# Another order of the jobs, and of the vector and pool work beside them, in a chain of routed feed-forward layers on one core

## The chip, the core and the metric

The kernel runs on one core of a Trainium2 chip. The metric is the device time of one execution in microseconds. Before the change it is 2493.7 us, the median of three executions (2493.61 to 2494.36).

The engines are named as the profile names them: PE (TensorE, matrix products; PEld is its weight load), DVE (VectorE), ACT (ScalarE), POOL (GpSimd) and SP (SyncE, which here only issues DMAs). Each engine works through its own list of instructions in order, and they meet by semaphores.

## The reference

64 sequences of 64 tokens with 512 features go through four layers. Layers 0, 2 and 3 have one form, with weights picked per sequence from three roles:

```python
h = gelu(x @ W_down[role] + b_down[role])       # 512 -> 256
y = x + h @ W_up[role] + b_up[role]             # 256 -> 512, residual
y = (y - mean(y)) * rsqrt(var(y) + 1e-5)
x = y * gamma[role] + beta[role]
```

Layer 1 is attention inside each sequence (512 features, one head) followed by two gelu blocks with 2048 hidden features, and a clip to [0, 1]:

```python
o = softmax(q @ k.T * scale) @ v @ Wp + bp
c = gelu(o @ cW1 + cb1) @ cW2 + cb2 + onehot(codes)
m = gelu(concat(o, c) @ mW1 + mb1) @ mW2 + mb2
x = clip(x + c + m, 0, 1)
```

All is float32. A product is computed as three products of a high and a low part (hi*hi, hi*lo, lo*hi), so each operand has to be split first: ACT copies it rounded (`_hi`), DVE subtracts (`_lo`).

## The kernel before

**Three blocks.** `first` is layer 0, then comes the core (layer 1, four passes of 1024 tokens), then `last`, layers 2 and 3 in one run of 18 jobs. `first` has 9 jobs.

**Jobs.** Sequences are sorted by role on the chip. A full job ("O") is 4 tiles of 128 tokens that all have one role, so its down weights are one matrix. A mixed job ("M") has 3 tiles, each with a role of its own; its down product (`pe_mix`) is made per tile with weights out of a table of all three roles (`wm`, split by `act_split_mixed` and `dve_split_mixed`), copied out by ACT (`act_mixed`) and turned back by PE (`pe_back`). The string `KINDS` gives the order of the kinds, here `OOOMOMOOM`, and with it job numbers, tiles in SBUF, the order of loads and the rows of each job. Jobs are numbered from 0 here; those of `last` run from 0 to 17, two rounds of the string.

**One job j, engine by engine.** The order is written out by hand in loops.
- PE: down product of j; up product of tile 0 of j-1; transposes of the inputs of j+1; up products of the other tiles of j-1. Two PSUM banks take turns for the up tiles, so the product of tile t waits until DVE has added tile t-2 to the residual (`y_done`).
- ACT: `act_moments` of j-2 (two small copies), gelu of both halves of the hidden layer, `act_norm` of the first two tiles of j-2, the hi part of the transposed inputs of j+1, the other tiles of `act_norm`, then the hi part of the down weights of j+2.
- DVE: lo part of the down weights of j+1, of the hidden halves of j, residual of tile 0 of j-1, lo part of the first half of the transposed inputs of j+1, residual of tile 1, second half, then statistics and residuals of the rest, and the aggregate.
- POOL: gathers the rows of job j+2 by indirect DMA, `pool_rstd_shift` of j-2, `pool_gain_shift` of j-3 (gamma and beta), and scatters j-3. ACT's `act_norm` waits for `pool_rstd_shift`.
- SP: down weights, the table `wm`, gains, and the inputs of the core.

**Round the edges.** At the end of `first`, PE transposes the core's inputs (`x_first`) between its last up products; ACT copies them (`xr`, `xc_hi`) once the rows of jobs 2, 3 and 4, which lie in the same SBUF, are stored. The value product of the core is copied by ACT to `x_tok`, where jobs 5 and 6 lie, so ACT first waits until their rows are stored (`for i in (4, 5)` in the scalar block, ahead of the loop over the passes). PE's second query product waits for the first two of these copies (`query`, `v_done`). In `last` the up weights of layer 3 take the place of layer 2's table `wm`, and layer 3's table is loaded after the ninth job's up products.

## Time and profile before

| what | value |
|---|---|
| median of three executions | 2493.7 us |
| profiled execution, device time | 2495.45 us |
| its span, first to last instruction | 2493.7 us |
| PE busy | 2405.3 us, 96% |
| DVE, ACT, POOL busy | 987.4, 874.2, 380.1 us |
| mean granted clock of TensorE | 0.99 |

The span is the stretch that the rows below count from; the execution's own time is 1.75 us more. In a row of the timeline the first number is the start, the second the busy time, and the bracket at the end is how long the engine was idle just before and what released it. Rows of several like instructions are merged (x3), and the second number is then the stretch they cover. "issue" means that the engine waited for nothing that the profile shows; loading a register from memory, as for the role of a tile, falls under it.

### The profile page before, as it was taken

What the parts mean: (1) busy time and instruction counts of PE and PEld (TensorE: products, weight loads), DVE (VectorE), ACT (ScalarE), POOL (GpSimd) and SP (SyncE); (2) the same over time, 40 slices, a digit from 0 to 9 for tenths busy, and PEclk for the clock granted to TensorE, in tenths of its full rate; (3) what the DMA queues carried; (4) which work ended last, traced back from release to release, by engine and by line L of the source; (5) the groups of instructions that cost most, each with busy time, mean ns of one, the idle gap of its engine ahead of it and who ended that gap; (6) DMA issues with size and microseconds to landing.
All of it is one profiled execution on the core that took longest, in us unless ns stands there. A gap on an engine that the chain in (4) does not pass through costs nothing.

```text
span 2493.7 us, 27695 instructions
## 1 busy us (share of the span) xinstructions
PE 2405.3 (96%) x11223; PEld 1990.1 (80%) x11223; DVE 987.4 (40%) x1361; ACT 874.2 (35%) x1242; POOL 380.1 (15%) x338
## 2 busy tenths in 40 slices
PE   8889999999999999999999999999999999989884
PEld 4768888888888888888888888888888888877773
DVE  4654434322324333223243332233433422266765
ACT  3464433222324332223243322232432222336553
POOL 2486000000000000000000000000100000018676
PEclk9999999999999999999999999999999999999997
DMA  5442111201111111111111121102111211242212
GB/s 184 175 164 103 68 51 51 81 38 51 51 68 51 51 51 70 49 51 45 75 51 48 40 81 51 51 29 90 51 37 49 85 51 34 85 152 72 77 60 89
DMA packets 42193, 175.39 MB, mean 70 GB/s; under 512 B 5698, under 2 KB 10306, under 8 KB 27476
## 3 DMA queue, kind: packets, MB, share of 16 engines
q1 hardware_dynamic: 35732, 139.02, 15.8%
q0 software_dynamic: 6336, 34.61, 3.6%
q8 instruction: 91, 1.49, 0.2%
q14 instruction: 34, 0.28, 0.0%
HBM read 145.82 MB, written 27.79 MB: 70 GB/s over the span
## 4 chain that ended last, share of the span: by engine, by line
PE 89%; DVE 4%; ACT 2%; issue 2%; POOL 1%; DMA 1%; ACTq 0%; SPq 0%; DVEq 0%; POOLq 0%
PE pair L71 22%; PE pair L73 22%; PE pair L72 22%; PE pair L1192 2%; PE pair L1191 2%; PE pair L1184 2%; PE pair L1183 2%; PE pair L1190 2%; PE pair L1182 2%; PE pair L1159 1%; PE pair L1143 1%; DVE last_xT_lo L714 1%; ACT pair L658 1%; PE pair L1227 1%; PE pair L612 1%
## 5 line engine op out<-in xcount | busy, mean ns | idle before, releaser
L1570 DVE TENSOR_TENSOR h_lo<-g,h_hi 128x512 fp32r<-128x512 f32 x256 | 179.1, 700 | 745.1 <-ACT h_hi L1381 744.9
L1379 ACT ACTIVATE g<-pair,bias_cols 128x512 f32<-128x512 f32 x256 | 176.6, 690 | 648.0 <-PE pair L73 411.6
L71 PE MATMUL pair<-h_hi,w_hiB 128*128 128x512 f32 x1024 | 399.0, 390 | 0.0
L73 PE MATMUL pair<-h_hi,w_loB 128*128 128x512 f32 x1024 | 398.4, 389 | 0.0
L72 PE MATMUL pair<-h_lo,w_hiB 128*128 128x512 f32 x1024 | 398.4, 389 | 0.0
L71 PE MATMUL pair<-o_hi,w_hiA 128*128 128x512 f32 x768 | 299.1, 390 | 0.0
L73 PE MATMUL pair<-o_hi,w_loA 128*128 128x512 f32 x768 | 298.8, 389 | 0.0
L72 PE MATMUL pair<-o_lo,w_hiA 128*128 128x512 f32 x768 | 298.7, 389 | 0.0
L1334 ACT ACTIVATE w_hiB<-w_raw 128x2048 fp32r<-128x2048 f32 x36 | 69.1, 1920 | 532.2 <-PE pair L73 504.9
L72 PEld LDWEIGHTS pair<-h_lo,w_hiB 128*128 128x128 f32 x1024 | 192.3, 188 | 39.8
L73 PEld LDWEIGHTS pair<-h_hi,w_loB 128*128 128x128 f32 x1024 | 192.2, 188 | 39.8
L71 PEld LDWEIGHTS pair<-h_hi,w_hiB 128*128 128x128 f32 x1024 | 192.2, 188 | 39.5
L1795 POOL COPY acc<-xr 128x1024 f32<-128x1024 f32 x16 | 16.0, 1038 | 1349.7 <-PE pair L1220 1349.7
L72 PEld LDWEIGHTS pair<-o_lo,w_hiA 128*128 128x128 f32 x768 | 144.2, 188 | 29.9
L73 PEld LDWEIGHTS pair<-o_hi,w_loA 128*128 128x128 f32 x768 | 144.2, 188 | 29.9
L71 PEld LDWEIGHTS pair<-o_hi,w_hiA 128*128 128x128 f32 x768 | 144.2, 188 | 29.7
L1381 ACT ACTIVATE h_hi<-g 128x512 fp32r<-128x512 f32 x256 | 162.0, 633 | 8.1
L1577 DVE TENSOR_TENSOR x_tok<-pair,x_tok 128x512 f32<-128x512 f32 x128 | 86.9, 689 | 185.8 <-PE pair L73 185.8
L1577 DVE TENSOR_TENSOR acc<-pair,acc 128x512 f32<-128x512 f32 x128 | 86.1, 688 | 141.9 <-PE pair L73 141.9
L1524 DVE TENSOR_TENSOR w_loA<-w_raw,w_hiA 128x2048 fp32r<-128x2048 f32 x36 | 83.3, 2313 | 67.2 <-ACT w_hiA L1334 67.2
L1524 DVE TENSOR_TENSOR w_loB<-w_raw,w_hiB 128x2048 fp32r<-128x2048 f32 x36 | 84.2, 2340 | 48.9 <-ACT w_hiB L1334 48.9
L1182 PE MATMUL pair<-o_hi,w_hiA 128*128 128x512 f32 x256 | 99.6, 389 | 0.0
(287 smaller groups left out, 4211.1 us busy)
## 6 DMA issues: line engine op xcount, KB each, us to landing
w_raw<-in_units_a SPq DMA_DIRECT2D x32, 1024.0 KB
w_raw<-in_units_b SPq DMA_DIRECT2D x32, 1024.0 KB, 4.8
w_raw<-in_units_c SPq DMA_DIRECT2D x16, 1024.0 KB, 4.8
x<-stage SPq DMA_DIRECT2D x32, 256.0 KB, 2.1
x_tok<-x SPq DMA_DIRECT2D x12, 512.0 KB, 7.3
last_wd_raw<-in_w_packed SPq DMA_DIRECT2D x12, 512.0 KB, 3.7
w_raw<-fold_m SPq DMA_DIRECT2D x4, 1024.0 KB
w_raw<-fold_v SPq DMA_DIRECT2D x4, 1024.0 KB, 5.6
```

The costliest lines, as they stand in the source:

```text
L71: pe.matmul(out, lh, rh, start=(i == 0), stop=False)
L72: pe.matmul(out, lh, rl, start=False, stop=False)
L73: last = pe.matmul(out, ll, rh, start=False, stop=(i == len(terms) - 1))
L1182: pe.matmul(bank[q], lh, rh, start=(i == 0), stop=False)
L1183: pe.matmul(bank[q], lh, rl, start=False, stop=False)
L1184: pe.matmul(bank[q], ll, rh, start=False, stop=False)
L1334: act.activation(w_hi[slot][:].rearrange("p k n -> p (k n)"), w_raw[i], ACT.Copy).then_inc(hi_done[slot], 1)
L1379: act.activation(g[q % 2][:], bank[q % 4], ACT.Gelu, bias=bias_at).then_inc(gelu_done, 1)
L1381: act.activation(h_hi[:, j, cols(n)], g[q % 2][:], ACT.Copy).then_inc(hhi_done, 1)
L1524: v.tensor_tensor(w_lo[slot][:].rearrange("p k n -> p (k n)"), w_raw[i], w_hi[slot][:].bitcast(F32).rearrange("p k n -> p (k n)"), ALU.sub ...
L1570: v.tensor_tensor(h_lo[:, j, cols(n)], g[q % 2][:], h_hi[:, j, cols(n)].bitcast(F32), ALU.subtract).then_inc(hlo_done, 1)
L1577: v.tensor_tensor(into[:, m, cols(n)], bank[4 + r % 4], into[:, m, cols(n)], ALU.add).then_inc(acc_done, 1)
```

## The change

It has seven parts.

1. `KINDS` becomes `OOOOMOMOM`: mixed jobs at the fifth, seventh and ninth place of each round. The places of the tiles in SBUF and the waits that name a job follow.
2. Mixed jobs: DVE adds the residual of tile 0 of j-1 ahead of the hidden halves, and ACT copies the transposed tiles ahead of all of `act_norm` (full jobs keep their order).
3. In `first`, POOL makes `pool_rstd_shift` ahead of the gathers.
4. In `first`, the full jobs 0, 1, 2, 3 and 5 are stored by SP with direct DMAs (`sp_store`); POOL scatters only jobs 4, 6, 7 and 8.
5. The splits of `wm` and of layer 3's up weights are spread over more places (`SPLIT_FIRST`, `SPLIT_LAST`, `early`, `middle`, `end`).
6. At the end of `first`, DVE makes all residuals of jobs 7 and 8 and the transposed tiles of the core first and the statistics of both jobs afterwards; ACT does `act_norm` of job 6 after all transposed tiles.
7. PE makes the down product of job 1 ahead of its wait for the folded weights. The last three jobs of `last` are now M, O, M, so POOL and DVE share the gains of job 15 as two tiles and one.

```diff
-KINDS = "OOOMOMOOM"
+KINDS = "OOOOMOMOM"
+    def sp_store(self, sp, j):
+        at = JOBS[j][1]
+        sp.wait_ge(self.add_done, self.GB[j + 1])
+        sp.dma_start(self.dst[0][P * at:P * (at + 1), :], self.x[j][:].rearrange("p t n -> p (t n)"))\
+          .then_inc(self.stored[self.stores[j]], 16)
...
+    SPLIT_FIRST = {1: ((MIX, 0, 0), (MIX, 0, 1)), 2: ((MIX, 0, 2),)}
...
+                if 4 <= j < 8:
+                    first.sp_store(sp, j - 4)
...
+            first.sp_store(sp, 5)
...
-                first.pe_job(pe, j, roles)
+                if j == 1:
+                    first.pe_down(pe, j)
+                    pe.wait_ge(fold_out[1], KD)
+                    first.pe_up(pe, j - 1, range(1), roles)
+                else:
+                    first.pe_job(pe, j, roles)
...
+            def act_job(ffn, j, splits):
+                roles, mixed, more = ffn.roles_of(act, j), not ffn.octet[j], j + 1 < ffn.NJ
+                if mixed:
+                    ffn.act_mixed(act, j)
+                if j >= 2:
+                    ffn.act_moments(act, j - 2)
+                for m in range(KB):
+                    ffn.act_gelu(act, j, m, roles)
+                if not more and ffn is first:
+                    return
+                if j >= 2 and not mixed:
+                    ffn.act_norm(act, j - 2, ffn.halves(j - 2)[0])
+                if more:
+                    for i in range(2):
+                        ffn.act_transposed(act, j + 1, i)
+                if j >= 2:
+                    ffn.act_norm(act, j - 2, range(0 if mixed else HALF, ffn.T[j - 2]))
+                if j + 2 < ffn.NJ and not (ffn is first and j == 0):
+                    ffn.act_split_down(act, ffn.units(j + 2))
+                for split_role, l, r in splits.get(j, ()):
+                    split_role(ffn, act, l, r)
...
+                if j and mixed:
+                    ffn.dve_residual(v, j - 1, 0)
+                for m in range(KB):
+                    ffn.dve_hidden(v, j, m)
+                if j and not mixed:
+                    ffn.dve_residual(v, j - 1, 0)
...
+            for j in (LAST - 1, LAST):
+                v.wait_ge(first.aggr_done, first.TB[j])
+                for t in range(first.T[j]):
+                    first.dve_statistics(v, j, t)
+                if j == LAST:
+                    split("B", 1)
+                first.dve_aggregate(v, j)
...
             for j in range(NP):
+                if j >= 2:
+                    first.pool_rstd_shift(pool, j - 2)
                 if j + 2 < NP:
...
-                if j >= 2:
-                    first.pool_rstd_shift(pool, j - 2)
                 if j >= 3:
                     first.pool_gain_shift(pool, j - 3)
-                    first.pool_scatter(pool, j - 3)
+                    if not first.octet[j - 3]:
+                        first.pool_scatter(pool, j - 3)
```

Three places where instructions move. The first is DVE in a mixed job of `first`, job 3 before (`first_x_197` is job 2, whose residual it adds).

```order
L688 TENSOR_TENSOR first_wd_lo_209<-first_wd_raw_211,first_wd_hi_207 128x1024
L722 TENSOR_TENSOR first_h_lo_217<-pair,first_h_hi_215 128x384 x2
L728 TENSOR_TENSOR first_x_197<-pair,first_x_197 128x512
L714 TENSOR_TENSOR first_xT_lo<-pair,first_xT_hi 128x2x4x128
L728 TENSOR_TENSOR first_x_197<-pair,first_x_197 128x512
```

The same in the changed kernel, where the mixed job is job 4 and `first_x_198` is job 3.

```order
L694 TENSOR_TENSOR first_wd_lo_208<-first_wd_raw_210,first_wd_hi_206 128x1024
L734 TENSOR_TENSOR first_x_198<-pair,first_x_198 128x512
L728 TENSOR_TENSOR first_h_lo_216<-pair,first_h_hi_214 128x384 x2
L720 TENSOR_TENSOR first_xT_lo<-pair,first_xT_hi 128x2x4x128
L734 TENSOR_TENSOR first_x_198<-pair,first_x_198 128x512
```

The residual of tile 0 (the first of the two rows on `first_x`) has moved ahead of the two hidden halves.

The second is POOL in `first`, from the gains of job 2 on, before (`first_x_203` is job 8, `columns` are the rstd and shift of a job).

```order
L789 TENSOR_TENSOR first_x_197<-first_x_197,first_gain_220 128x1024 x2
L795 ISA
L795 TENSOR_TENSOR first_x_197<-first_x_197,first_gain_220 128x1024 x2
L824 DMA x<-first_x_197,oct_rank_90 2304x2048
L809 DMA first_x_203<-in_x,tok_src_100 128x512
L809 DMA first_x_203<-in_x,tok_src_101 128x512
L809 DMA first_x_203<-in_x,tok_src_102 128x512
L774 TENSOR_TENSOR columns<-columns 128x4
L776 TENSOR_TENSOR columns<-columns 128x4
```

And in the changed kernel.

```order
L795 TENSOR_TENSOR first_x_197<-first_x_197,first_gain_220 128x1024 x2
L801 ISA
L801 TENSOR_TENSOR first_x_197<-first_x_197,first_gain_220 128x1024 x2
L780 TENSOR_TENSOR columns<-columns 128x3
L782 TENSOR_TENSOR columns<-columns 128x3
L815 DMA first_x_203<-in_x,tok_src_100 128x512
L815 DMA first_x_203<-in_x,tok_src_101 128x512
L815 DMA first_x_203<-in_x,tok_src_102 128x512
```

The scatter of job 2 is gone from POOL, and the `columns` stand ahead of the gather.

The third is DVE at the end of `first`, before (`first_x_202` is job 7, `first_x_203` job 8, `xc_lo` the core's transposed tiles).

```order
L732 BN_STATS stats<-first_x_202 128x6 x2
L739 BN_AGGR mean_var<-stats 128x2 x4
L1524 TENSOR_TENSOR w_loA<-w_raw,w_hiA 128x2048
L728 TENSOR_TENSOR first_x_203<-pair,first_x_203 128x512
L1530 TENSOR_TENSOR xc_lo<-pair,xc_hi 128x4x128
L728 TENSOR_TENSOR first_x_203<-pair,first_x_203 128x512
L1530 TENSOR_TENSOR xc_lo<-pair,xc_hi 128x4x128
L728 TENSOR_TENSOR first_x_203<-pair,first_x_203 128x512
L1530 TENSOR_TENSOR xc_lo<-pair,xc_hi 128x4x128 x2
```

And in the changed kernel.

```order
L1519 TENSOR_TENSOR w_loA<-w_raw,w_hiA 128x2048
L1525 TENSOR_TENSOR xc_lo<-pair,xc_hi 128x4x128
L734 TENSOR_TENSOR first_x_203<-pair,first_x_203 128x512
L1525 TENSOR_TENSOR xc_lo<-pair,xc_hi 128x4x128
L734 TENSOR_TENSOR first_x_203<-pair,first_x_203 128x512
L1525 TENSOR_TENSOR xc_lo<-pair,xc_hi 128x4x128 x2
L734 TENSOR_TENSOR first_x_203<-pair,first_x_203 128x512
L738 BN_STATS stats<-first_x_202 128x6 x4
L745 BN_AGGR mean_var<-stats 128x2 x4
```

The aggregate of job 7 has moved behind the last residual of job 8.

## Rows read from the trace of the kernel before

**Rows 1.** Stretches: length, busy PE, PEld, DVE, ACT, POOL, clock, DMA share, GB/s.
```profile
0.00:192.39 192.39, 161.65 (x741) 121.18 (x742) 109.03 (x227) 93.89 (x158) 104.71 (x142) 0.96 0.49 177
...
2200.00:2464.00 264.00, 236.00 (x1229) 192.84 (x1227) 169.94 (x281) 144.28 (x258) 181.54 (x123) 0.98 0.25 87
...
2360.00:2380.00 20.00, 15.94 (x86) 13.41 (x86) 14.00 (x24) 11.16 (x20) 11.34 (x9) 0.91 0.09 27
```
**Rows 2.** Waits of PE from 2160 us on: total, times, longest.
```profile
PE pair L608 <- DVE last_x L728: 14.5, 14, 2.4
```
**Rows 3.** Timeline, PE, from a mixed job's start to the next job's.
```profile
2308.85 0.39 PE L564 MATMUL pair<-last_wm,last_xT_hi 128*128 x1 [0.74 <-issue]
2319.72 0.50 PE L608 MATMUL pair<-last_up_rows,last_pick 128*128 x1 [0.65 <-DVE last_x L728]
2322.71 0.50 PE L608 MATMUL pair<-last_up_rows,last_pick 128*128 x1 [1.10 <-DVE last_x L728]
2324.80 0.47 PE L71 MATMUL pair<-last_xT_hi,last_wd_hi 128*128 128x512 f32 x1 [0.21 <-issue]
```
**Rows 4.** Timeline, ACT in the same job.
```profile
2318.38 1.51 ACT L679 ACTIVATE last_x<-last_x,columns 128x512 f32<-128x512 f32 x2
...
2319.79 1.92 ACT L649 ACTIVATE last_xT_hi<-pair 128x1024 fp32r<-128x1024 f32 x2
```
**Rows 5.** Timeline, PE, where layer 3 begins.
```profile
2350.04 0.50 PE L608 MATMUL pair<-last_up_rows,last_pick 128*128 x1 [1.41 <-DVE last_x L728]
...
2367.59 0.50 PE L608 MATMUL pair<-last_up_rows,last_pick 128*128 x1 [0.96 <-DVE last_x L728]
2372.58 0.58 PE L564 MATMUL pair<-last_wm,last_xT_hi 128*128 x1 [3.10 <-DVE last_wm L700]
```
**Rows 6.** Timeline, DVE, splits without and beside POOL's work.
```profile
2224.81 1.19 DVE L700 TENSOR_TENSOR last_wm<-last_wm 128x1024 fp32r<-128x1024 f32 x1
2353.89 2.71 DVE L700 TENSOR_TENSOR last_wm<-last_wm 128x1024 fp32r<-128x1024 f32 x1
```
**Rows 7.** Timeline, PE, `first` to the core.
```profile
53.70 0.47 PE L71 MATMUL pair<-first_xT_hi,first_wd_hi 128*128 128x512 f32 x1 [1.65 <-issue]
81.36 0.50 PE L608 MATMUL pair<-first_up_rows,first_pick 128*128 x1 [3.88 <-DVE first_x L728]
88.41 0.39 PE L564 MATMUL pair<-first_wm,first_xT_hi 128*128 x1 [1.76 <-DVE first_wm L700]
149.36 0.50 PE L71 MATMUL pair<-first_xT_hi,first_wd_hi 128*128 128x512 f32 x1 [3.36 <-DVE first_xT_lo L714]
...
192.39 0.47 PE L71 MATMUL pair<-xc_hi,w_hiA 128*128 128x512 f32 x1 [2.07 <-DVE xc_lo L1530]
212.32 0.48 PE L71 MATMUL pair<-xc_hi,w_hiA 128*128 128x512 f32 x1
```
**Rows 8.** Timeline, POOL: first half of the gains, full and mixed job.
```profile
158.62 4.77 POOL L789 TENSOR_TENSOR first_x<-first_x,first_gain 128x1024 f32<-128x1024 f32 x2 [0.54 <-issue]
174.17 3.79 POOL L789 TENSOR_TENSOR first_x<-first_x,first_gain 128x512 f32<-128x512 f32 x3 [2.23 <-issue]
```
**Rows 9.** Timeline, ACT: the table in `first`, and a norm behind POOL.
```profile
75.15 1.06 ACT L632 ACTIVATE first_wm<-first_wm 128x1024 fp32r<-128x1024 f32 x1 [11.30 <-DMA first_wm<-in_w_packed]
143.90 1.52 ACT L679 ACTIVATE first_x<-first_x,columns 128x512 f32<-128x512 f32 x2 [2.99 <-POOL columns L776]
```
**Rows 10.** Timeline round the first query product: POOL, ACT.
```profile
187.63 1.04 POOL L774 TENSOR_TENSOR columns<-columns 128x4 f32<-128x4 f32 x1 [0.43 <-ACT columns L673]
...
209.03 0.60 ACT L1356 ACTIVATE x_tok<-pair 128x512 f32<-128x512 f32 x1 [1.26 <-PE pair L73]
```
**Rows 11.** Landing of the scatters of mixed jobs in `first` (line 829, 9 DMAs).
```profile
DMA to landing us min/median/max: 2.8/6.1/8.0
```
**Rows 12.** Timeline, the tail: PE, DVE.
```profile
2455.69 0.50 PE L608 MATMUL pair<-last_up_rows,last_pick 128*128 x1 [2.39 <-DVE last_x L728]
2466.85 3.45 DVE L747 TENSOR_TENSOR last_x<-last_x,last_gain 128x512 f32<-128x512 f32 x2 [1.18 <-issue]
```

More of the change, by code:

```diff
@@ L1582, in finished, with dve_job @@
                     v.tensor_scalar(stage[:, SPOT[s == SB - 1][t], :], bank[F_BANK[s == SB - 1][t]], 0.0, 1.0, ALU.max, ALU.min).then_inc(fin_done, 1)
+            def dve_job(ffn, j, early=None, middle=None, end=None):
+                mixed, more = not ffn.octet[j], j + 1 < ffn.NJ
+                if more:
+                    ffn.dve_split_down(v, ffn.units(j + 1))
+                if early:
+                    early()
+                if j and mixed:
[4 more added lines that the diff above has]
+                    ffn.dve_residual(v, j - 1, 0)
+                if more:
+                    ffn.dve_transposed(v, j + 1, 0)
+                if j:
+                    ffn.dve_residual(v, j - 1, 1)
+                if more:
+                    ffn.dve_transposed(v, j + 1, 1)
+                if middle:
+                    middle()
+                if j:
+                    ffn.dve_statistics(v, j - 1, 0)
+                    for t in range(2, ffn.T[j - 1]):
+                        ffn.dve_residual(v, j - 1, t)
+                        ffn.dve_statistics(v, j - 1, t - 1)
+                    ffn.dve_statistics(v, j - 1, ffn.T[j - 1] - 1)
+                    ffn.dve_aggregate(v, j - 1)
+                if end:
+                    end()
             routed.dve_tables(v)
@@ new lines, in _ @@
+            transposed(0, range(4, 5))
+            first.dve_residual(v, LAST, 0)
+            transposed(0, range(5, 6))
+            first.dve_residual(v, LAST, 1)
+            transposed(0, range(6, TT))
+            first.dve_residual(v, LAST, 2)
+            for j in (LAST - 1, LAST):
[5 more added lines that the diff above has]
+                first.dve_aggregate(v, j)
@@ L1830, in _ @@
             last.pool_rstd_shift(pool, j - 1)
-            last.pool_gain_shift(pool, j - 2, range(1))
+            last.pool_gain_shift(pool, j - 2, range(HALF))
             last.pool_rstd_shift(pool, j)
```

150 lines of the change are left out of this document (32 added, 118 removed).

## The prediction

> **What bounds the kernel now.** I read the busy time by stretch first. The reader is to see that PE is idle for 30.7 us ahead of the core's first query product at 192.39 us and for 28.0 us between 2200 and 2464, and that nothing is left for PE in the last 29.7 us of the span of 2493.7 [rows 1]. Between 192.39 and 2200 PE is never idle, and the change touches that stretch only at its start. So the gain can only come from some 88 us, a part of which is the start of the program, before any data is there. The view of waits then says who holds PE in `last`: DVE's residual adds, 14 times, 14.5 us in total [rows 2]. A timeline of one mixed job shows the pattern, the same in all nine of them: the up products of tiles 2 and 3 each wait for a residual, 0.65 and 1.10 us, and the job takes 15.95 us from its start to the next one's [rows 3]. Two places stand out beside it: the beginning of layer 3, where PE waits on residuals and then 3.10 us on the split of the table [rows 5], and `first`, with stalls of 1.65, 3.88, 1.76 and 3.36 us [rows 7]. In a 20 us window round the 3.10 us stall the granted clock is 0.91 of full, 2.4 GHz, so 20 x 0.09 = 1.8 us are lost to PE's lower clock level after it stood still [rows 1]. I charge 1.8 us to each stall of over 3 us.
>
> **Mixed jobs.** With the residual of tile 0 ahead of the hidden halves, tile 2 of the up product finds it done (0.65 gone). Tile 3 waits for residual 1, which on DVE stands behind the first transposed half, and that one behind ACT's copy. ACT starts its two norm tiles at 2318.38 and the copy at 2319.79, so dropping the norms brings the copy 1.41 us forward [rows 4], and all behind it with it. The two stalls sum to 1.75; 1.41 of it goes, about 0.4 stays before tile 3. The norms then end where they ended, and nobody but POOL waits for them. Bounds: 0.65 if only the residual counts, 1.75 if all goes. Five such jobs of `last` lie on PE's path (the sixth belongs to the tail): 7.0 us. Two of `first`: 2.8 us.
>
> **Layer 3's beginning.** The stalls of 1.41, 0.96 and 3.10 us [rows 5] come from two or three splits in a row on DVE. Spread out, one stands in a place, and the table is used a job later. I take 5.5 + 1.8 (clock) - 0.3 (a remainder at the first up product, for which the third up split is just in time) = 7.0 us. A split costs DVE 1.19 us alone and 2.71 beside POOL's gains [rows 6], so the bounds are 4 and 8.
>
> The Trainium skill (SBUF — State Buffer, section "Who interferes with whom") says that a DVE operation with two inputs in SBUF and a GpSimd one that reads SBUF lock each other out for a whole instruction. The 2.71 beside 1.19 agrees with it. By the rule a split could wait for one of POOL's 2.4 us instructions, and at three places (jobs 3, 9 and 12) each stall could be 1.2 us longer, which would make the whole gain 3.6 us smaller; I do not count that.
>
> **The order of kinds.** A mixed job behind two full ones starts after 0.74 us of idle time, a job in the other neighbourhoods after 0.21 [rows 3]. Each round has one such place instead of two: 2 x 0.5 = 1.0 us in `last`.
>
> **The tail.** Behind the last residual DVE multiplies and adds for 9 tiles, and its first two instructions take 3.45 us because POOL works beside it [rows 12]. Now it has 8 tiles: two instructions fewer, at most 3.45 us. The 2.39 us stall of PE ahead of it [rows 12] loses about 1.5, the residual being ahead of the hidden halves. Against it: the roles of a mixed job load in 2.23 us instead of 0.54 [rows 8] on POOL and DVE. POOL gets this back, because job 14 is full and has one scatter instead of three. I take 2.5, bounds 1 and 4.
>
> `last` gives 7.0 + 7.0 + 1.0 + 2.5 = 17.5 us.
>
> **`first` up to the query product.** The wait for the folded weights moves behind a product that needs none of them: 1.6 of 1.65 [rows 7]. The stalls of 3.88 and 1.76 come from the table: ACT waits 11.30 us for it and everything behind ACT is late [rows 7, 9]. The new code waits at the same place and then makes two splits instead of one (1.06 more), but the table's last split is needed a job later (1.76 gone), and POOL's 1 MB gather, which shared the DMA engines with it, now stands behind `pool_rstd_shift` and comes later. About 2.1 of the 3.88 stay: 3.5 us, bounds 1.5 and 5; a shorter stall also spares most of the low clock, 1.5. Mixed jobs: 2.8.
>
> The stall of 3.36 us at 149.36 is POOL's: ACT's norm stood 2.99 us behind `columns` [rows 7, 9], which stood behind a scatter and three gathers. They are moved. But POOL remains nearly full. The gains of a full job take 0.5 to 0.8 + 2 x 4.77 = 10.3 us, of a mixed job 2.2 + 2 x 3.79 = 9.8 [rows 8], `columns` 1.3 and a mixed job's three gathers 3.8. Through job 6 that is 1.3 + 3.8 + 10.3 = 15.4 us against a mixed job's 15.95 - 1.41 = 14.5, and job 4 is no better. Carried along, `columns` come about 1 us late in job 5 and 2 us late in job 7. So 3.0 of 3.36 + 1.8 stay, 2.2 go. With the 1.6, 3.5, 1.5 and 2.8 that is 11.6.
>
> ACT's copies of the core's inputs wait until job 4's rows are stored. It is a mixed job now, stored by POOL: gains 9.8, three scatters 3.8, landing 6.1 in the middle [rows 8, 11]. It lands some 4 us after ACT wants it (range 0 to 7). Part is slack, since PE's last up products of `first` follow the copies anyway; I charge 1.0. The query product, call its start Q, comes 10.6 us earlier than 192.39.
>
> **The new wait behind Q.** This is what I think takes most of that back. Before, POOL's `columns` of job 7 ran at 187.63, so Q - 4.8 [rows 10]. Now its aggregate stands on DVE behind job 8's last residual: residual, four statistics and the aggregate at about 0.6 each as the like-sized copies of [rows 10], 3.5 us in sum, and ACT's two small copies 0.5. So `columns` start at Q + 4.0, end at Q + 5.3, and only then POOL turns to the gains of job 6: roles 1.6 to 2.2, six instructions 7.5 (up to 10 beside the split of the value weights), three scatters. The last is issued at Q + 17.4 to Q + 20.5 and lands 2.8 to 8.0, mostly 6.1 us later [rows 8, 11]: Q + 24.5. ACT is not allowed to copy the first value product before that. PE's second query product needs two such copies; before, it started at Q + 19.9 and the second copy at Q + 16.6 [rows 7, 10]. Now it starts at 24.5 + 1.3 = Q + 25.8: a stall of 5.9 us (bounds 1 and 10), and 1.8 for the clock. Queued behind ACT's wait are both value copies, the softmax and the second query's copies, so nothing else can fill PE. This costs 7.7, and `first` gives 10.6 - 7.7 = 2.9.
>
> SP's stores cost nothing that I see: they stand behind the last down weights in SP's queue, each waits for POOL's adds, and the load of the core's inputs behind the third is needed only two jobs later. If that cover were gone, each microsecond would count in full.
>
> **Sum.** 17.5 + 2.9 = 20.4 us. Against the profiled execution: its span 2493.7 becomes 2473.3, its own time 2495.45 becomes 2475.05. The median shown, 2493.7, is 1.75 under that execution, so I forecast **2473.3 us**.
>
> **Rivals.**
> - *The wait behind Q does not reach PE* (the landing takes 2.8 us or POOL gets to job 6 sooner). For it: slack of 3 us in the trace, and a landing range that begins at 2.8. Against it: `columns` alone move by almost 9 us. Then 20.4 + 7.7 = 28.1, giving 2465.6. Chance 0.16.
> - *POOL or ACT stays the bound and the mixed jobs gain little.* The stalls come back as late norms: seven times 1.41 = 9.9 us less, 2483.2. For it: 15.4 us of POOL work beside 14.5 in `first`. Against it: in `last` POOL has no scatters in layer 2, and in both layers its work stays under the job's length. Chance 0.13.
> - *Slower than before: POOL pushed far into the core.* From Q + 5 on POOL has 33 us of gains, and behind them come its scatters and the four copies that the attention output waits for. If DVE locked it out so that this work took 1.7 times as long (the DVE split of [rows 6] took 2.3 times), the copies would come 23 us late and only some 2 us of that are covered: 2473.3 + 21 = 2494 or more, so it decides from that factor on. Against it: before, the same work beside the same DVE instructions was hardly longer. Chance 0.03.
> - My forecast keeps 0.68, with its own range 2469 to 2478, by the bounds of the stall behind Q and of layer 3's beginning.
>
> The range that should hold 8 times in 10 goes from 2464 (a little under the first rival) to 2484 (a little over the second). About 0.2%, 5 us, is what a measurement can tell from no change. Faster by more 0.95; within it 0.02, from mishaps that eat 15 us without the third rival; slower 0.03.
>
> **What would show it.** PE's rows in mixed jobs: no wait at tile 2 and about 0.4 at tile 3, 14.5 us from start to start. No wait of 3 us on the table in layer 3. In `first`, Q near 182 and, behind it, a PE wait of about 6 us at the second query product, with ACT idle before its first `x_tok` copy and released by the scatter of job 6. The tail 2 to 3 us shorter from the last matmul's job on. I am wrong if that wait is missing, if ACT's norms wait for `columns` in `last`, or if mixed jobs still take 15.9 us.

## The result, and the profile after

| kernel | median us | its runs | ratio to before, 95% interval |
|---|---|---|---|
| before | 2493.65 | 2492.71 to 2494.36 | |
| changed | 2478.32 | 2478.06 to 2479.39 | 0.994, 0.9922 to 0.9957 |

The change makes the kernel 15.3 us faster by the medians and 17.2 us by the profiled executions (spans 2493.7 and 2476.5). The forecast was 2473.3 us with a range of 2464 to 2484. So sign and range were right and the forecast 5 us too low. Of the 5 us, 3.2 are misses in the stretches below; the other 1.8 come from the 1.75 us that the forecast took off because the profiled execution before lay that much over its median, while that of the changed kernel (2478.22) lies on its median. The sum hides larger errors of both signs, and the table below shows where. It cuts the spans at seven starts of PE's work: P (first down product of `first`), M8 (mixed products of its last job), Q and Q2 (first and second query product), D (down product of job 2 of `last`), M17 (mixed products of its last job) and the end. Each entry is the difference of two such starts.

| us | P | P to M8 | M8 to Q | Q to Q2 | Q2 to D | D to M17 | M17 to end |
|---|---|---|---|---|---|---|---|
| before | 37.38 | 127.88 | 27.13 | 19.93 | 2009.37 | 223.13 | 48.88 |
| changed | 36.17 | 119.22 | 30.48 | 22.01 | 2011.67 | 208.15 | 48.80 |
| e1_plain_mixed | 36.16 | 120.44 | 28.38 | 22.03 | 2010.18 | 216.25 | 47.36 |
| e2_split_early | 36.30 | 112.85 | 30.53 | 22.03 | 2011.61 | 208.04 | 48.74 |
| e3_scatter6_first | 36.90 | 119.52 | 30.51 | 19.91 | 2009.93 | 208.55 | 48.78 |
| e4_dve_tail | 36.24 | 119.41 | 30.46 | 22.02 | 2011.87 | 208.01 | 45.79 |
| e5_before_mixed | 36.35 | 127.19 | 27.13 | 19.90 | 2009.77 | 217.80 | 46.96 |
| e6_scatter4_early | 36.66 | 118.09 | 27.48 | 22.03 | 2010.79 | 209.10 | 48.85 |
| e7_up_bunched | 37.38 | 118.26 | 31.06 | 22.02 | 2010.26 | 208.69 | 48.83 |
| e8_pool_first_undone | 37.60 | 120.19 | 30.89 | 22.02 | 2011.58 | 208.15 | 49.27 |
| e9_last_splits | 37.31 | 119.84 | 30.62 | 22.02 | 2010.25 | 205.88 | 48.98 |
| e10_same | 36.20 | 119.42 | 30.29 | 22.03 | 2011.77 | 208.13 | 48.76 |
| c1_four_moves | 37.53 | 111.45 | 27.82 | 19.89 | 2010.05 | 209.10 | 45.76 |
| c2_all_moves | 36.65 | 111.65 | 27.26 | 19.91 | 2010.35 | 205.23 | 45.15 |

Against before, the changed kernel gains 1.2 us at P, 8.7 up to M8 and 15.0 between D and M17. It loses 3.4 between M8 and Q, 2.1 behind Q and 2.3 on the way to D. The tail gives 0.1.

The waits of PE in `last` come first, as in [rows 2]: what PE waited for, the total, how often, the longest, from 2140 to 2470 us of the changed kernel.

```profile
PE pair L71 <- DVE last_xT_lo L720: 5.8, 2, 5.5
PE pair L614 <- DVE last_x L734: 3.8, 6, 0.8
PE pair L570 <- DVE last_wm L706: 3.5, 2, 2.2
```

The residuals held PE 14 times for 14.5 us and now hold it 6 times for 3.8. A mixed job of `last` shows it (PE, all rows with an idle time, to answer [rows 3]):

```profile
2302.85 0.38 PE L570 MATMUL pair<-last_wm,last_xT_hi 128*128 x1 [0.21 <-DVE last_xT_lo L720]
2315.30 0.50 PE L614 MATMUL pair<-last_up_rows,last_pick 128*128 x1 [0.60 <-DVE last_x L734]
2317.35 0.47 PE L71 MATMUL pair<-last_xT_hi,last_wd_hi 128*128 128x512 f32 x1 [0.17 <-issue]
```

The wait at tile 2 is gone, 0.60 stays at tile 3, and from start to start it is 14.50 us instead of 15.95.

What was not foreseen in `first` is the table's third split. The timeline of DVE, POOL and PE there:

```profile
91.52 6.82 DVE L706 TENSOR_TENSOR first_wm<-first_wm 128x1024 fp32r<-128x1024 f32 x1
87.88 4.78 POOL L795 TENSOR_TENSOR first_x<-first_x,first_gain 128x1024 f32<-128x1024 f32 x2
92.61 4.63 POOL L801 TENSOR_TENSOR first_x<-first_x,first_gain 128x1024 f32<-128x1024 f32 x2
98.59 0.58 PE L570 MATMUL pair<-first_wm,first_xT_hi 128*128 x1 [5.57 <-DVE first_wm L706]
```

DVE starts the split at 91.52, while POOL is in the second of its four gain instructions, and ends it at 98.34, 1.10 us behind the end of the fourth (92.61 + 4.63 = 97.24). It was let in neither at 92.61 nor between the two adds. PE stands 5.57 us for it.

The same split in `last` got in after one instruction (timeline of DVE and POOL; PE waited 1.29 us):

```profile
2246.72 2.67 DVE L706 TENSOR_TENSOR last_wm<-last_wm 128x1024 fp32r<-128x1024 f32 x1
2245.90 5.73 POOL L801 TENSOR_TENSOR last_x<-last_x,last_gain 128x1024 f32<-128x1024 f32 x2
```

Here POOL's two adds are about 1 us longer than the 4.63 above: POOL gave way between them. The place in layer 3 is like it: the split starts 0.04 us behind POOL's first add and takes 3.42 us, and PE waits 2.20 us. Before, two splits stood in a row there, 4.26 us together beside POOL's adds, and PE waited 3.10 us [rows 5]. The changed kernel (DVE, POOL, PE), and then DVE before:

```profile
2369.32 3.42 DVE L706 TENSOR_TENSOR last_wm<-last_wm 128x1024 fp32r<-128x1024 f32 x1
2369.28 5.69 POOL L801 TENSOR_TENSOR last_x<-last_x,last_gain 128x1024 f32<-128x1024 f32 x2
2373.01 0.38 PE L570 MATMUL pair<-last_wm,last_xT_hi 128*128 x1 [2.20 <-DVE last_wm L706]
```

```profile
2368.05 4.26 DVE L700 TENSOR_TENSOR last_wm<-last_wm 128x1024 fp32r<-128x1024 f32 x2
```

The granted clock from 2360 to 2380 us is 0.91 in the changed kernel, the same as before [rows 1].

The entry of the core, where ACT waits for the stores of jobs 2, 3 and 4 (POOL, SP's queue, ACT, PE):

```profile
163.61 0.97 POOL L835 DMA_INDIRECT x<-first_x,tok_rank  x1 [0.30 <-issue]
163.07 0.32 SPq L1056 DMA_DIRECT2D w_raw<-fold_v  x1
171.80 0.60 ACT L1360 ACTIVATE xr<-pair 128x512 f32<-128x512 f32 x1 [6.81 <-DMA x<-first_x,tok_rank]
175.24 0.79 PE L614 MATMUL pair<-first_up_rows,first_pick 128*128 x1 [8.03 <-DVE first_x L734]
```

Job 4's last scatter is issued at 163.61, just behind two loads of 1 MB each by SP, and ACT's copy starts 8.2 us later. ACT waits 6.81 us, DVE's copies wait for ACT, the residual of job 7 stands behind them on DVE, and PE waits 8.03 us.

Behind Q (which is at 185.87; POOL, ACT, PE):

```profile
189.54 1.02 POOL L780 TENSOR_TENSOR columns<-columns 128x4 f32<-128x4 f32 x1 [13.95 <-ACT columns L679]
203.90 0.97 POOL L835 DMA_INDIRECT x<-first_x,tok_rank  x1 [0.30 <-issue]
206.65 0.60 ACT L1370 ACTIVATE x_tok<-pair 128x512 f32<-128x512 f32 x1 [5.88 <-issue]
207.88 0.47 PE L71 MATMUL pair<-xc_hi,w_hiA 128*128 128x512 f32 x1 [1.84 <-ACT x_tok L1370]
```

The chain that the prediction described is there: `columns` at Q + 3.7, the last scatter at Q + 18.0, ACT's copy behind it. But the copy starts 2.75 us behind the last issue, where 6.1 had been taken for the landing alone. The profile names no releaser for this copy ("issue"); that it waited for the scatter is shown by e3 below.

The tail (ACT, POOL, DVE), to answer [rows 12]:

```profile
2448.92 2.93 ACT L685 ACTIVATE last_x<-last_x,columns 128x512 f32<-128x512 f32 x4 [5.78 <-POOL columns L782]
2457.63 1.30 POOL L780 TENSOR_TENSOR columns<-columns 128x3 f32<-128x3 f32 x1
2459.74 1.21 POOL L835 DMA_INDIRECT out_rows<-last_x,tok_dst  x1 [0.28 <-DVE last_x L757]
2468.57 0.96 POOL L835 DMA_INDIRECT out_rows<-last_x,tok_dst  x1 [0.30 <-issue]
2453.14 5.68 DVE L753 TENSOR_TENSOR last_x<-last_x,last_gain 128x512 f32<-128x512 f32 x4
```

From M17 (2427.70) on POOL's longest pause is 2.51 us, at 2451.40, where the profile has it wait for ACT's norm of job 15, which had waited for POOL's own `columns`. Seven scatters stand in a row from 2459.74 to 2469.53, and DVE has ended its last instruction by 2464.8. Before, DVE bounded the tail: POOL waited for its adds twice, 2.96 and 3.40 us, the second time here (POOL before):

```profile
2483.10 0.97 POOL L829 DMA_INDIRECT out_rows<-last_x,tok_dst  x1 [3.40 <-DVE last_x L751]
```

### The profile page after: what moved, and what is told of

It is laid out like the page before. It is cut to its first block, busy times and chain, and to the rows that moved or that the text cites. A ratio compares the mean times of both kernels' runs of the same rounds, so it can differ in the third digit from the quotient of the medians.

```text
span 2476.5 us, 27698 instructions
## 1 busy us (share of the span) xinstructions
PE 2398.9 (97%) x11223; PEld 1990.3 (80%) x11223; DVE 993.3 (40%) x1359; ACT 873.8 (35%) x1242; POOL 374.6 (15%) x333
## 4 chain that ended last, share of the span: by engine, by line
PE 87%; POOL 3%; issue 3%; DVE 3%; ACT 2%; DMA 1%; POOLq 0%; SPq 0%; ACTq 0%; DVEq 0%
PE pair L71 22%; PE pair L73 22%; PE pair L72 22%; PE pair L1203 2%; PE pair L1202 2%; PE pair L1195 2%; PE pair L1194 2%; PE pair L1201 2%; PE pair L1193 2%; PE pair L1170 1%; PE pair L1154 1%; POOL last_x L801 1%; DVE last_xT_lo L720 1%; PE pair L1238 1%; ACT pair L664 1%
```

## The experiments

All ratios are to the kernel before. Differences to the changed kernel are of medians (2478.32 us), those of stretches are from the table. The interval of a ratio is about 4 us to either side, so it does not settle a difference of 2 or 3 us between two changed kernels. What does is that their executions do not overlap with the eight of the changed kernel (2478.06 to 2479.39, e10 counted in), except in e7, and above all the stretches. "..." marks lines of an edit that are left out.

**e1_plain_mixed: the order in a mixed job, taken out.**

```diff
-                if j and mixed:
-                    ffn.dve_residual(v, j - 1, 0)
                 for m in range(KB):
                     ffn.dve_hidden(v, j, m)
-                if j and not mixed:
+                if j:
                     ffn.dve_residual(v, j - 1, 0)
...
-                if j >= 2 and not mixed:
+                if j >= 2:
                     ffn.act_norm(act, j - 2, ffn.halves(j - 2)[0])
...
-                    ffn.act_norm(act, j - 2, range(0 if mixed else HALF, ffn.T[j - 2]))
+                    ffn.act_norm(act, j - 2, range(HALF, ffn.T[j - 2]))
```

> The changed kernel with one part undone: in mixed jobs the residual of tile 0 stands behind the hidden halves again, and ACT's first norms ahead of the transposed copies. Theory A (the copies come forward by the two norms, 1.41 us, and by the residual): a mixed job of `last` takes 15.9 us from start to start instead of 14.5, with two waits of about 0.65 and 1.1 us at tiles 2 and 3. Five of them in `last` give 7.0 us, two in `first` 1.4 to 2.8: 2478.3 + 8.4 to 9.8 = 2487 to 2488 us. Theory B (the shorter jobs come from the order of the kinds and the moved splits, not from this order within a job): jobs stay at 14.5 to 15.0 and the time at 2478 to 2481.

2483.07 us, ratio 0.996 (0.9945 to 0.9974), 4.8 us slower than the changed kernel. PE in the job shown above:

```profile
2304.37 0.39 PE L570 MATMUL pair<-last_wm,last_xT_hi 128*128 x1 [0.21 <-DVE last_xT_lo L720]
2315.24 0.50 PE L614 MATMUL pair<-last_up_rows,last_pick 128*128 x1 [0.64 <-DVE last_x L734]
2318.22 0.50 PE L614 MATMUL pair<-last_up_rows,last_pick 128*128 x1 [1.08 <-DVE last_x L734]
2320.28 0.47 PE L71 MATMUL pair<-last_xT_hi,last_wd_hi 128*128 128x512 f32 x1 [0.16 <-issue]
```

Both waits are back and the job takes 15.91 us. The time lies between the ranges of the two theories. Theory A holds for the mixed jobs of `last`: D to M17 is 8.1 us longer, five times 1.4 and 1.0 in the job behind D (a matter of the clock, last section). It fails for `first`, where the time up to Q2 is 0.9 us shorter than with the order: 1.2 lost up to M8, 2.1 won behind it. The entry, bound by POOL and the stores, decides there. The tail gives 1.4 back, since POOL ends it in any case, and 1.5 from Q2 to D is clock (below).

**e5_before_mixed: the same order alone, put into the kernel before** (the edit of e1 turned round, on the old loops).

> The kernel before with one part of the change alone: in mixed jobs the residual of tile 0 ahead of the hidden halves and ACT's norms behind the transposed copies; kinds, splits and POOL's order as they were. Theory A (1.41 us for each mixed job on PE's path): jobs of `last` at 14.5 us, six of them between the core and the tail at most: 7.0 to 8.5 us in `last`; in `first` up to 2.8 more, of which POOL's late norm in job 8 may take some: 2493.7 - 7 to - 11 = 2483 to 2487 us. Theory B (the order pays only with the new places of the mixed jobs): under 4 us gained, 2490 us or more.

2488.42 us (2484.56 to 2490.3 in 9 runs), ratio 0.9977 (0.9967 to 0.9987): 5.2 us gained by the medians, between the two theories. The profiled execution (2486.87) gained 8.6: 1.0 at P, 0.7 up to M8, 5.3 from D to M17 and 1.9 in the tail, less 0.4 from Q2 to D. Five jobs are 1.4 us shorter each, but PE waits 1.23 and 0.98 us in the job ahead of M17, and in `first` the gain is nearly nothing, for this reason (ACT, PE):

```profile
141.81 1.52 ACT L679 ACTIVATE first_x<-first_x,columns 128x512 f32<-128x512 f32 x2 [6.27 <-POOL columns L776]
147.28 0.79 PE L71 MATMUL pair<-first_xT_hi,first_wd_hi 128*128 128x512 f32 x1 [6.64 <-DVE first_xT_lo L714]
```

The norm's wait for POOL grew from 2.99 to 6.27 us and PE's from 3.36 to 6.64. In the old order of POOL, what a mixed job wins beside it is handed back at POOL's next `columns`.

**e8_pool_first_undone: POOL's part of `first`, taken out.**

```diff
-                if 4 <= j < 8:
-                    first.sp_store(sp, j - 4)
...
-            first.sp_store(sp, 5)
...
-                if j >= 2:
-                    first.pool_rstd_shift(pool, j - 2)
...
                     first.pool_gather(pool, j + 2)
+                if j >= 2:
+                    first.pool_rstd_shift(pool, j - 2)
                 if j >= 3:
                     first.pool_gain_shift(pool, j - 3)
-                    if not first.octet[j - 3]:
-                        first.pool_scatter(pool, j - 3)
...
+                    first.pool_scatter(pool, j - 3)
```

> The changed kernel with POOL's part of `first` undone: the columns (rstd and shift) stand behind the gathers again, and POOL, not SP, stores jobs 0 to 3 and 5 by scatters. Theory A (POOL is full from job 5 on, so each microsecond put on it lands on PE): columns 1.3 to 3.8 us later each time, four scatters of 1.1 us more ahead of job 4's, so ACT's norms wait 3 to 5 us in jobs 5 to 7 and the core's inputs come 4 to 6 us later: 2482 to 2486 us. Theory B (the table's split and not POOL sets the pace of `first`): under 2 us, 2478 to 2480.

2480.99 us, ratio 0.9945 (0.9929 to 0.9962), 2.7 us slower, of which 1.4 already stands at P. Neither theory fits. A wait of 3.44 us at POOL's `columns` appears as in theory A (PE at 127.58), but the wait of 5.57 us on the table is gone (DVE, POOL, PE):

```profile
95.50 1.22 DVE L706 TENSOR_TENSOR first_wm<-first_wm 128x1024 fp32r<-128x1024 f32 x1
95.56 5.75 POOL L801 TENSOR_TENSOR first_x<-first_x,first_gain 128x1024 f32<-128x1024 f32 x2
127.58 0.57 PE L570 MATMUL pair<-first_wm,first_xT_hi 128*128 x1 [3.44 <-DVE first_xT_lo L720]
```

DVE's split starts 0.06 us ahead of POOL's adds and takes 1.22 us, and POOL's adds are the longer ones. So the split's 6.82 us belong to where its start meets POOL's row of gains. Parts 3 and 4 of the change are undone together here, so what each is worth by itself is not shown.

**e2_split_early: the table's third split in `first`, moved.**

```diff
-    middle={2: lambda: first.dve_split_mixed(v, 0, 0), 3: lambda: first.dve_split_mixed(v, 0, 2)}.get(j),
+    early={3: lambda: first.dve_split_mixed(v, 0, 2)}.get(j),
+    middle={2: lambda: first.dve_split_mixed(v, 0, 0)}.get(j),
```

> The changed kernel with one instruction moved: in `first`, DVE splits the table's third role at the start of job 3, ahead of the hidden halves, instead of behind its transposed halves. Theory A (the split of 6.82 us at 91.52 is held by POOL's gains of job 0, four instructions back to back from 87.88, and costs PE its 5.57 us wait before the mixed job and the low clock behind it): the split takes about 1.2 us, the wait of 5.57 is gone or under 0.5, the mixed products take 4.6 instead of 5.6 us, and the time falls by 5 to 7 us, less what the entry of the core takes back (PE waits there 8.03 us for a scatter, and POOL has no slack of its own): if POOL was not the bound from job 3 on, all is kept, 2472 us; Theory B (POOL's chain of gains sets the entry): the earlier PE waits longer at the entry and the time falls by 2 us or less, 2476 to 2478.

2472.94 us, ratio 0.9916 (0.9900 to 0.9933), 5.4 us faster than the changed kernel. P to M8 is 6.4 us shorter, 4.3 up to the first mixed job's start and 2.1 in that job (14.50 instead of 16.61 us; behind the wait of 5.57 us the granted clock is 0.73 from 98 to 108 us of the changed kernel). Every later stretch is the same within 0.15. The first row holds two splits, the moved one among them:

```profile
84.32 2.33 DVE L706 TENSOR_TENSOR first_wm<-first_wm 128x1024 fp32r<-128x1024 f32 x2
94.44 0.38 PE L570 MATMUL pair<-first_wm,first_xT_hi 128*128 x1 [1.08 <-issue]
```

Theory A. That M8 to Q stays at 30.53 shows that POOL's chain moved with PE and did not hold it: POOL had waited for DVE's aggregates, which stood behind the split. Its wait ahead of the `columns` of job 2 goes from 8.82 to 2.06 us.

**e6_scatter4_early: job 4's gains ahead of job 3's.**

```diff
-        sp.wait_ge(self.add_done, self.GB[j + 1])
+        sp.wait_ge(self.add_done, self.GB[5 if j == 3 else j + 1])
...
+                if j == 6:
+                    first.pool_gain_shift(pool, 4, base=first.GB[3])
+                elif j == 7:
+                    first.pool_scatter(pool, 4, first.GB[3] + MT)
+                    first.pool_gain_shift(pool, 3, base=first.GB[3] + MT)
-                if j >= 3:
+                elif j >= 3:
                     first.pool_gain_shift(pool, j - 3)
-                    if not first.octet[j - 3]:
-                        first.pool_scatter(pool, j - 3)
```

> The changed kernel with POOL's gains of job 4 (mixed) ahead of those of job 3, and job 4's three scatters right behind the columns of job 5; job 3 is stored by SP as before, once its adds are done. Theory A (ACT's copies of the core's inputs, and PE's 8.03 us wait at 175.24 behind them, wait for the stores of jobs 3 and 4, and POOL's order decides when they land): the scatters are issued 9 us earlier, the last store wanted lands near 168 instead of 171.8, and the first query product comes 3 to 4 us earlier. The wait behind it moves along. 2474 to 2476 us. Theory B (the copies are bound elsewhere, or the columns of job 5, now 0.8 us later, cost what is won): 2478 to 2480.

2474.40 us, ratio 0.9916 (0.9899 to 0.9932), 3.9 us faster than the changed kernel. POOL's last scatter of job 4, SP's store of job 3, ACT's first copy and PE:

```profile
151.97 0.97 POOL L835 DMA_INDIRECT x<-first_x,tok_rank  x1 [0.30 <-issue]
162.43 0.33 SPq L493 DMA_DIRECT2D x<-first_x  x1
167.35 0.60 ACT L1360 ACTIVATE xr<-pair 128x512 f32<-128x512 f32 x1 [3.00 <-DMA x<-first_x]
170.79 0.80 PE L614 MATMUL pair<-first_up_rows,first_pick 128*128 x1 [4.22 <-DVE first_x L734]
```

Theory A: PE's wait is 3.8 us shorter, M8 to Q 3.0 us. ACT now waits for job 3's store. PE's wait at M8 also falls, from 1.74 to 0.50 us.

**e3_scatter6_first: job 6's scatters ahead of job 7's columns.**

```diff
-            first.pool_rstd_shift(pool, LAST - 1)
             first.pool_gain_shift(pool, LAST - 2)
             first.pool_scatter(pool, LAST - 2)
+            first.pool_rstd_shift(pool, LAST - 1)
```

> The changed kernel with POOL's two small instructions on job 7's columns moved behind the gains and the scatters of job 6. They waited for an aggregate at 189.5 us, 3.7 us behind the first query product, and held the gains of job 6 with them. Theory A (ACT's first value copy waits for this scatter, and PE's 1.84 us wait at the second query product with the low clock behind it comes from nothing else): the gains start about 6 us earlier, the wait goes and 2 to 3.5 us are gained, 2475 to 2476 us. Theory B (the wait at the second query product has another cause, or the late columns of job 7 hold ACT in their turn): no change, 2478 us, or up to 2 us slower.

2475.88 us, ratio 0.9925 (0.9909 to 0.9942), 2.4 us faster than the changed kernel. POOL and ACT:

```profile
185.33 3.79 POOL L795 TENSOR_TENSOR first_x<-first_x,first_gain 128x512 f32<-128x512 f32 x3 [8.76 <-ACT first_x L685]
197.54 0.97 POOL L835 DMA_INDIRECT x<-first_x,tok_rank  x1 [0.30 <-issue]
203.02 1.13 ACT L1370 ACTIVATE x_tok<-pair 128x512 f32<-128x512 f32 x2
```

ACT no longer waits, Q to Q2 is 19.91 us as before the change, and Q2 to D falls by 1.7 as well. Theory A.

**e4_dve_tail: job 15's gains all on DVE.**

```diff
...
-            last.pool_gain_shift(pool, j - 2, range(HALF))
...
-            last.dve_gain_shift(v, j - 2, range(HALF, last.T[j - 2]), 0)
-            rest = last.T[j - 2] - HALF
+            last.dve_gain_shift(v, j - 2, range(last.T[j - 2]), 0)
+            rest = last.T[j - 2]
```

> The changed kernel with the gains of job 15 (three tiles, mixed) all on DVE; POOL does none of them. Theory A (POOL's chain bounds the tail: role loads 2.5 us, four instructions 6.3 us, columns of job 17 at 2457.6 and then seven scatters at 1.27 us each): POOL is free for the columns of job 17 some 5 us earlier, DVE isn't locked out and takes 0.6 us an instruction, 20 of them from 2450.9 to 2463, and the last scatters are issued by 2467.5 instead of 2469.5: 2 us gained, 2476.3 us (2475 to 2477). Theory B (DVE's two instructions more cost what POOL's absence gives): 2478 to 2480.

2475.90 us, ratio 0.9927 (0.9911 to 0.9944), 2.4 us faster than the changed kernel; M17 to the end is 3.0 us shorter.

```profile
2466.14 0.96 POOL L833 DMA_INDIRECT out_rows<-last_x,tok_dst  x1 [0.30 <-issue]
2454.77 2.49 DVE L753 TENSOR_TENSOR last_x<-last_x,last_gain 128x512 f32<-128x512 f32 x4
```

The four multiplications of job 16 take 2.49 us instead of 5.68, and the last scatter is issued 2.4 us sooner. Theory A: POOL's chain bounded the tail.

**e7_up_bunched: layer 3's up splits in a row again.**

```diff
-            EARLY = {9: lambda: last.dve_split_up(v, 1, 0), 12: lambda: last.dve_split_mixed(v, 1, 1)}
+            EARLY = {12: lambda: last.dve_split_mixed(v, 1, 1)}
...
-                      9: lambda: last.dve_split_up(v, 1, 1), 11: lambda: last.dve_split_mixed(v, 1, 0),
+                      9: lambda: [last.dve_split_up(v, 1, r) for r in range(ROLES)], 11: lambda: last.dve_split_mixed(v, 1, 0),
...
-            END = {9: lambda: last.dve_split_up(v, 1, 2)}
+            END = {}
```

> The changed kernel with layer 3's three splits of the up weights in a row again, in the middle of DVE's job 9 (and ACT's in its job 9). Theory A (they held PE by residuals that stood behind them, 1.41 and 0.96 us in the kernel before): the two waits return, 2.4 us, and the time is 2480.5 us (2480 to 2483, more if POOL's gains hold a split). Theory B (they were hidden anyway and only the table's split counted): no change, 2478.3.

2479.41 us, ratio 0.9941 (0.9924 to 0.9957), 1.1 us slower by the medians, but its executions (2478.29 to 2480.36) overlap with the changed kernel's, so the difference is not clear of noise, and the time lies between the two theories. D to M17 is only 0.5 longer.

```profile
2341.23 0.50 PE L614 MATMUL pair<-last_up_rows,last_pick 128*128 x1 [1.22 <-DVE last_x L734]
2344.07 0.50 PE L614 MATMUL pair<-last_up_rows,last_pick 128*128 x1 [0.95 <-DVE last_x L734]
2374.57 0.38 PE L570 MATMUL pair<-last_wm,last_xT_hi 128*128 x1 [1.73 <-DVE last_wm L706]
```

The two waits return as theory A has it, 2.2 us, but most of it comes back at the table: the wait is 0.5 shorter, and the job behind it, from its mixed products to the next down product, takes 14.5 us instead of 16.0. That 1.5 is the low clock, missing here.

**e9_last_splits: the table splits of `last`, moved.**

```diff
-            EARLY = {9: lambda: last.dve_split_up(v, 1, 0), 12: lambda: last.dve_split_mixed(v, 1, 1)}
-            MIDDLE = {2: lambda: last.dve_split_mixed(v, 0, 1), 3: lambda: last.dve_split_mixed(v, 0, 2),
-                      9: lambda: last.dve_split_up(v, 1, 1), 11: lambda: last.dve_split_mixed(v, 1, 0),
-                      12: lambda: last.dve_split_mixed(v, 1, 2)}
-            END = {9: lambda: last.dve_split_up(v, 1, 2)}
+            EARLY = {3: lambda: last.dve_split_mixed(v, 0, 2), 9: lambda: last.dve_split_up(v, 1, 0),
+                     12: lambda: last.dve_split_mixed(v, 1, 2)}
+            MIDDLE = {2: lambda: last.dve_split_mixed(v, 0, 1),
+                      9: lambda: last.dve_split_up(v, 1, 1), 11: lambda: last.dve_split_mixed(v, 1, 0)}
+            END = {9: lambda: last.dve_split_up(v, 1, 2), 11: lambda: last.dve_split_mixed(v, 1, 1)}
```

> The changed kernel with the table splits of `last` moved as the one of `first` was: the third role of layer 2's table at the start of DVE's job 3, the second role of layer 3's at the end of job 11 and the third at the start of job 12, none in the middle of jobs 3 and 12. Theory A (splits of 2.67 and 3.42 us, held by POOL's gains, cost PE 1.29 us at 2249.7 and 2.20 us at 2373.0, and mixed products at the lower clock, 6.09 instead of 4.58 us, behind the second): both waits go or fall under 0.5 us, the low clock goes with them, and 3.5 to 5 us are gained, 2473.5 to 2475 us. Theory B (the split ahead of the hidden halves is held by POOL too, or holds the hidden halves back, so that PE waits at its up products instead): 2477 to 2480.

2475.88 us, ratio 0.9926 (0.9909 to 0.9943), 2.4 us faster than the changed kernel, between the two theories. PE at the two places:

```profile
2250.47 0.38 PE L570 MATMUL pair<-last_wm,last_xT_hi 128*128 x1 [0.72 <-issue]
2372.57 0.38 PE L570 MATMUL pair<-last_wm,last_xT_hi 128*128 x1 [0.92 <-issue]
```

D to M17 is 2.3 us shorter, less than theory A's 3.5 to 5. Of the waits of 1.29 and 2.20 us, 0.72 and 0.92 are left, and DVE no longer releases them. The low clock behind the second is gone, but the job behind D took 16.3 instead of 15.4 us.

**e10_same: the changed kernel again.**

> The changed kernel unchanged, as a measure of what differs from run to run: so far the first product of the profiled executions starts between 36.2 and 37.6 us, and the core takes 1985.2 or 1986.9 us, the latter with 1.6 us of lower clock behind a wait of 1.84 us that nearly all have. Theory A (both are chance, of the execution): stretches between equal waits repeat within 0.1 us, these two may come out otherwise; median 2478.3 within 1 us. Theory B (they belong to the kernel's code): 36.2 us and 1986.9 us again.

2478.43 us, ratio 0.9938 (0.9922 to 0.9955). All stretches of the two profiled executions repeat within 0.2 us, P and the one behind Q2 among them. That speaks for theory B, but it is one repeat. Kernels with the same code ahead of P have it at 36.2 to 37.6 us, and in other kernels the executions do differ: e6 has one of 2471.53 us at a mean clock of 0.991 beside three of 2474.26 to 2474.70 at 0.990, and e7's four rise from 2478.29 to 2480.36 us as the clock falls from 0.991 to 0.989. So chance, of the execution, is not excluded.

**c1_four_moves and c2_all_moves: moves together.** The first kernel has the edits of e2, e3, e4 and e6, the second that of e9 too.

> Four of the single edits in one kernel: third role of `first`'s table split at the start of job 3, job 4's gains and scatters ahead of job 3's gains, job 6's scatters ahead of job 7's columns, job 15's gains all on DVE. Theory A (they act at four different places and their gains add up, the low clock behind the second query product counted once): 2478.3 - 6.4 - 3.0 - 2.1 - 1.65 - 3.0 = 2462 us, range 2461 to 2465. Theory B (POOL is the bound of `first` behind all of them, so that an earlier PE only waits longer for the stores at the entry): 2466 to 2470.

2462.77 us, ratio 0.9873 (0.9856 to 0.9889).

> The four moves and the table splits of `last` moved as well. Theory A (all add up): another 3.5 to 5 us below the kernel with four moves, 2457 to 2461 us. Theory B (a POOL shifted by the other moves now meets the splits at their new places): within 1 us of the four moves.

2458.64 us, ratio 0.986 (0.9843 to 0.9876), 35.0 us faster than before and 19.7 faster than the changed kernel. Theory A holds for both. In `first` the windows from 40 to 181 us, with the columns of [rows 1], show it for the kernel with all moves and then for the changed one:

```profile
40.00:181.00 141.00, 131.60 (x677) 107.12 (x676) 89.35 (x148) 81.16 (x144) 86.70 (x61) 0.98 0.48 172
```

```profile
40.00:181.00 141.00, 122.57 (x633) 100.24 (x632) 83.71 (x128) 74.32 (x133) 79.10 (x55) 0.95 0.46 164
```

PE works 9.0 us more in the same stretch, at 0.98 instead of 0.95 of the full clock.

## Why the prediction came out as it did

- **Mixed jobs, 7.0 us in `last`: right.** 15.95 became 14.50 us per job, and e1 loses 7.0 again in five jobs. The 0.4 us left at tile 3 were 0.60.
- **Mixed jobs, 2.8 us in `first`: wrong.** e1 shows no gain up to Q2. The working itself said that POOL is nearly full there and that the entry hangs on its scatter; I should have counted nothing.
- **Layer 3's beginning 7.0 and kinds 1.0: right in sum, in part by luck.** D to M17 gave 15.0, as forecast; without the mixed jobs' 7.0 that leaves 8.0, of which 1.0 lies ahead of job 9 and 7.0 behind it. Inside the 7.0, the 1.8 us of clock did not come as charged: PE still waits 2.20 us on the table, the clock round it is 0.91 as before, and the job behind it takes 16.02 us. On the other side the working left out a wait of 0.99 us on a residual at 2352.90, which has gone too. What each part gives isn't settled: e7 shows that spreading the up splits removes 2.2 us of waits, but with the clock only 0.5 us net.
- **The table in `first`, 5.0 us with the clock: failed, the largest error in `first`.** The stall of 3.88 shrank to 0.31 and 0.96, better than forecast, and the 1.76 at the table became 5.57. The failed step is the sentence "at three places (jobs 3, 9 and 12) each stall could be 1.2 us longer ... I do not count that". The place in job 3 cost 6.4 us (e2), and the 1.5 us of clock that were to be spared are part of them. The Trainium skill's rule named there (SBUF — State Buffer, "Who interferes with whom") points at the right pair of instructions, and its whole instruction fits the 2.67 us of the split in `last`. In `first` the split was locked out for more than two.
- **Fold wait, 1.6 us: right.** From P to the next down product it is 14.08 instead of 16.32 us, and the next job gives 0.3 back (13.97 instead of 13.66).
- **POOL's stall in job 8, "2 us late": right.** PE waited 1.74 us there. Of wait and clock 3.0 us had been left in the sum, so this was a little dear.
- **Entry, charged 1.0: failed.** It "lands some 4 us after ACT wants it" became 6.81 us. And "part is slack" was wrong: from ACT's first copy (171.80) to Q it is 14.1 us, almost filled by ACT's sixteen copies and a split, so hardly any of it was hidden. M8 to Q lost 3.4 us; e6 gets 3.0 of them back by POOL's order alone.
- **Behind Q, 5.9 + 1.8: mechanism right, size wrong.** The chain is as written and e3 shows it, but the landing took under 2.75 us where I took the median of [rows 11], 6.1, and the wait was 1.84. The clock was 1.7. Q came 4.1 us later than the forecast's 181.8, mostly by the table and the entry, and Q to Q2 took 22.0 us instead of 25.8. These two errors cancel, which is luck: Q2 came 4.4 us earlier than before, where 10.6 - 5.9 = 4.7 had been forecast.
- **Tail, 2.5: failed, 0.1.** "Now it has 8 tiles: two instructions fewer" looked at DVE. PE did end its part 1.0 us sooner, but POOL's chain took over the end: `columns` of job 17 at 2457.63, then seven scatters in 9.8 us. "POOL gets this back, because job 14 is full" was the wrong step. e4 gains 3.0 there. The order in the mixed job did shorten this stretch where the work was shared as before (e5, 46.96 us).
- **Not in the sum:** 1.2 us at P and minus 0.65 between the end of the core and D, where PE waited 5.52 instead of 4.88 us.

The forecast was 20.4, the profiled executions gave 17.2: tail minus 2.4, Q2 minus 0.3, and between Q2 and D minus 0.5, where 1.8 was charged for the clock and 2.3 lost.

What stays open: what parts 6 and 7 of the change are worth by themselves, since neither was undone alone; why P lies between 36.2 and 37.6 us in kernels whose code up to there is the same, and what in a kernel decides whether the low clock follows a given wait (below). Kernels in which POOL's and DVE's instructions meet at set distances were not run, so when a waiting DVE instruction is let in between two of POOL's is not known.

## What to carry to other kernels

Where POOL and DVE both work on SBUF, look up for every DVE instruction that the matmul engine waits for which row of POOL's long instructions it will start in, and place it in POOL's idle time; one split moved ahead by some 6 us gained more than any other edit here. Where an engine is nearly full, count a gain beside it as nothing until the trace shows that the next thing it delivers isn't waited for; the same reorder gave 7 us in one block and none in the other. For each store that a later stage waits for, ask what else stands ahead of its issue: here columns, and gains of a job whose store was less urgent.

## What the runs showed of the hardware

- **A lockout may last longer than one instruction.** The same 128x1024 split took 1.19 us alone, 2.67 and 3.42 beside POOL's gains, and 6.82 when it began in the second of four. Where it began 0.06 us ahead of POOL's adds it took 1.22.
- **Equal waits, unequal clocks.** In the changed kernel and in e1 PE waits 1.84 and 1.86 us ahead of the second query product. The windows of the changed kernel (208 to 220 us) and of e1 (207 to 220 us) behind it:

```profile
208.00:220.00 12.00, 12.00 (x46) 9.71 (x47) 4.53 (x4) 5.36 (x8) 11.12 (x7) 0.86 0.16 67
```

```profile
207.00:220.00 13.00, 12.98 (x57) 10.79 (x58) 4.62 (x5) 7.21 (x10) 12.12 (x8) 1.00 0.20 82
```

  The granted clock is 0.86 in one and 1.00 in the other. 12 x 0.14 = 1.7 us is what Q2 to D differs by once PE's wait at D (5.52 and 5.73 us) is taken off. Behind the table's wait in layer 3 it is 1.5 us or nothing, behind D 1.0 or nothing. Together that is 4 us, as much as most single edits here, and in the repeat (e10) it came again, while executions of one kernel differ by 3.2 us in e6 and 2.1 in e7, the faster ones at the higher mean clock. So a median difference of 2 us between two orders of the work may be the clock's alone, and only the stretches tell.
- **Landings.** In the changed kernel ACT's copy started 2.75 us behind the start of a mixed job's last scatter at 203.90, and the DMA engines were busy for 0.47 of that time (191 GB/s). Behind the scatter at 163.61 it was 8.2 us, at a busy share of 0.82 (311 GB/s), with two loads of 1 MB issued just ahead. In e7 the two loads were issued just behind the scatter (164.02 and 164.81 against 163.79), and it was still 7.66 us. So the wait goes with the traffic, and the loads need not stand ahead; no run leaves them out.
